# Router logits with the weights as the stationary operand, in a strip of 16 of 128 columns, and two transposes per half of the tokens

## The reference

```python
x = x + tanh(g_xattn) * xattn(layernorm(x), ctx, mask, W, b)
h = layernorm(x)
logits = h @ w_router                      # 2048 x 8
top_logits, top_idx = top_k(logits, 2)
scores = softmax(top_logits)
# each token goes to its 2 experts: silu(h @ fc1[:, :256]) * (h @ fc1[:, 256:]) @ fc2
moe = sum over the 2 experts of scores * expert(h)
shared = silu(h @ gate_w) * (h @ up_w) @ down_w      # inner width 512
x = x + tanh(g_ffn) * (moe + shared)
```

## Time and profile before

| what | value |
|---|---|
| three timed runs | 239.44, 240.22, 240.24 us (median 240.22) |
| span of the profiled execution | 237.5 us |
| median of the runs less that span | 2.7 us |
| PE busy | 222.3 us, 94% |
| DVE / ACT / POOL busy | 72% / 55% / 53% |
| TensorE clock in the profile's slices | 9 tenths or more in all 40 |

### The profile page before, as it was taken

The page is one execution under the profiler, slowest core; times in us unless marked ns, Lnnn a source line. Parts: engine busy times, 40 slices in busy tenths (PEclk is TensorE's granted clock), DMA queues, the critical chain, the costliest instruction groups (busy, mean ns, idle before and its releaser), DMA issues.

```text
span 237.5 us, 5283 instructions
## 1 busy us (share of the span) xinstructions
PE 222.3 (94%) x1425; PEld 193.7 (82%) x1425; DVE 171.8 (72%) x513; ACT 129.8 (55%) x316; POOL 125.1 (53%) x177
## 2 busy tenths in 40 slices
PE   7688999999989999999599999999999999999984
PEld 7578999978778888888488888888888888888763
DVE  0977897797767799999977665665665665664794
ACT  2465788773647645464125656656656656655320
POOL 1688898464777887887701334334334334334600
PEclk9999999999999999999999999999999999999999
DMA  5999950000121225322242443343343332008877
GB/s 154 286 362 406 404 199 3 0 0 25 45 94 67 74 85 179 136 91 92 67 123 65 135 127 94 96 125 96 88 127 92 94 120 68 37 38 267 288 238 310
DMA packets 18131, 32.05 MB, mean 135 GB/s; under 512 B 3046, under 2 KB 9323, under 8 KB 18104
## 3 DMA queue, kind: packets, MB, share of 16 engines
q1 hardware_dynamic: 14096, 22.28, 29.8%
q0 software_dynamic: 3408, 8.46, 9.5%
q10 hardware_dynamic: 600, 0.97, 1.3%
HBM read 19.95 MB, written 12.67 MB: 137 GB/s over the span
## 4 chain that ended last, share of the span: by engine, by line
PE 46%; POOL 8%; issue 6%; DMA 2%; DVE 2%; SPq 0%; DVEq 0%; ACT 0%; POOLq 0%
PE bank L994 38%; POOL rows L388 6%; PE bank L1245 4%; PE bank L1265 3%; POOL ew_lo L243 2%; DMA rows<-hrows,slot 1%; DMA hrows<-rows 1%; DVE act_lo L630 1%; DVE acc L710 0%; PE bank L1179 0%; DVE act L929 0%; DVE acc L966 0%; SPq L280 0%; ACT act L581 0%; DVEq L62 0%
## 5 line engine op out<-in xcount | busy, mean ns | idle before, releaser
L430 POOL DMA_INDIRECT parts<-y_out,dst x39 | 38.7, 991 | 69.9 <-DVE dst L923 66.1
L388 POOL DMA_INDIRECT rows<-hrows,slot x32 | 35.0, 1095 | 12.3 <-issue 12.3
L929 DVE TENSOR_TENSOR act<-act,bank 128x256 f32<-128x256 f32 x39 | 16.4, 421 | 34.5 <-issue 25.0
L581 ACT ACTIVATE act<-bank 128x256 f32<-128x256 f32 x39 | 15.0, 384 | 37.1 <-PE bank L994 37.1
L994 PE MATMUL bank<-ew_hi,m_xt_hi 128*128 x78 | 30.9, 396 | 0.1
L994 PE MATMUL bank<-ew_hi,m_xt_lo 128*128 x78 | 30.8, 395 | 0.0
L994 PE MATMUL bank<-ew_lo,m_xt_hi 128*128 x78 | 30.7, 394 | 0.0
L994 PE MATMUL bank<-ew_hi,act_hi 128*128 x78 | 25.2, 323 | 0.1
L994 PE MATMUL bank<-ew_hi,act_lo 128*128 x78 | 21.9, 281 | 0.0
L994 PE MATMUL bank<-ew_lo,act_hi 128*128 x78 | 21.9, 281 | 0.0
L443 ACT ACTIVATE act_hi<-act 128x512 fp32r<-128x512 f32 x16 | 10.1, 630 | 21.2 <-DVE act L690 9.1
(11 more groups left out here) (186 smaller groups left out, 655.6 us busy)
## 6 DMA issues: line engine op xcount, KB each, us to landing
ew_raw<-in_chunks SPq DMA_DIRECT2D x12, 512.0 KB, 10.7
hrows<-rows SPq DMA_DIRECT2D x39, 130.0 KB, 2.1
low_buf<-parts SPq DMA_DIRECT2D x4, 512.0 KB, 4.6
high_buf<-parts SPq DMA_DIRECT2D x4, 512.0 KB, 3.9
acc<-in_x SPq DMA_DIRECT2D x7, 256.0 KB, 4.6
sw_raw<-in_chunks SPq DMA_DIRECT2D x3, 512.0 KB, 9.0
out<-acc SPq DMA_DIRECT2D x3, 512.0 KB, 3.0
rows<-pad_rows SPq DMA_DIRECT2D x9, 130.0 KB
```

What stands on the lines that cost most here:

```text
L388: pool.indirect_dma_start(out=rows, out_offset=bass.IndirectOffsetOnAxis(ap=slot[:, h, k, i:i + 1], axis=0), in_=hrows[:, HT * h + i, :], ...
L430: pool.indirect_dma_start(out=parts, out_offset=bass.IndirectOffsetOnAxis(ap=dst[:, t:t + 1], axis=0), in_=y_out[:, t % SLOTS, :], in_offs ...
L581: a.activation(act[:, p, 0:I], M_H[p][:, 0:I], ACT.Silu).then_inc(s["m_sil"], 1)
L929: TT(act[:, p, 0:I], act[:, p, 0:I], M_H[p][:, I:2 * I], ALU.mult).then_inc(s["m_prod"], 1)
```

## The change

The router weights become the stationary operand. `wr` is widened from 16 to 176 columns per half of the features (WZ is 48), all zeros but for 16 columns in the middle; POOL writes the zeros at the start. For the group at place `at_` (0 to 3) in its half a window of 128 columns of it is taken, so that the 16 weight columns lie at 16 x `at_`. The 256 tokens of the group move past it, once as `ht_hi` and once as `ht_lo`, for each of the two halves of the features: four matmuls of 256 columns a group. All four groups of a half add into the same 128x256 of bank 6, each into its own 16 partitions, since the others' columns are zero there.

The logits then lie with experts on partitions and tokens along the row. DVE copies the 64x256 of them to SBUF (`cut_logits`), the PE turns them with two transposes (`turn_logits`), and DVE reads the turned ones (`read_logits`), now with an index order of its own. `turn_logits(0)` stands within `gate(0)`, behind its first three matmuls, and `turn_logits(1)` within `gate(3)`. `cut_logits(0)` takes the place of `read_logits(0)`, and that moves behind `softmax_out(6)`.

```diff
+HG = NG // NH
+WZ = 2 * E * (HG - 1)
...
-        wr = sb("wr", [P, K, 2 * E], F32R)
+        wr = sb("wr", [P, K, WZ + P], F32R)
+        lgt = sb("lgt", [HG * 2 * E, GN])
...
+            pool.memset(wr[:].bitcast(F32), 0.0).then_inc(s["wr_z"], 1)
             pool.wait_ge(s["const_m"], 1)
...
-            hi(wr[:, :, 0:E], wr_raw, "wr_h")
+            after(a, "wr_z", 1)
+            hi(wr[:, :, WZ:WZ + E], wr_raw, "wr_h")
...
-            lo(wr[:, :, E:2 * E], wr_raw, wr[:, :, 0:E], "wr_l")
+            lo(wr[:, :, WZ + E:WZ + 2 * E], wr_raw, wr[:, :, WZ:WZ + E], "wr_l")
...
+            def cut_logits(h):
+                after(v, "lg_ps", HG * (h + 1))
+                after(v, "lg_turned", h)
+                v.tensor_copy(lgt[:], bank[6][0:HG * 2 * E, 0:GN]).then_inc(s["lg_cut"], 1)
+
             def read_logits(h):
-                after(v, "lg_ps", (NG // NH) * (h + 1))
-                lp = bank[6][:, HT * h * 2 * E:HT * (h + 1) * 2 * E].rearrange("p (t e) -> p t e", e=2 * E)
-                v.tensor_copy(lgx[:], lp).then_inc(s["lg_read"], 1)
+                after(v, "lg_turned", h + 1)
+                lp = bank[6][:, GN:GN + HT * 2 * E].rearrange("p (j g e) -> p g j e", j=GT, g=HG)
+                v.tensor_copy(lgx[:].rearrange("p (g j) e -> p g j e", j=GT), lp).then_inc(s["lg_read"], 1)
...
                 if t == NG - 1:
                     after(v, "const_c", 7)
-                    read_logits(0)
+                    cut_logits(0)
                 softmax_out(t - 1)
...
                 if t == NG - 1:
+                    read_logits(0)
                     first_choice(0)
...
+            cut_logits(1)
             read_logits(1)
...
             def router(g):
                 after(pe, "ht_l", g + 1)
+                at_ = g % HG
+                if at_ == 0:
+                    after(pe, "lg_cut", g // HG)
+                w_ = slice(WZ - 2 * E * at_, WZ - 2 * E * at_ + P)
+                for k in range(K):
+                    for x_ in (ht_hi, ht_lo):
+                        ins = pe.matmul(bank[6][:, 0:GN], wr[:, k, w_], x_[:, k, g * GN:(g + 1) * GN],
+                                        start=at_ == 0 and k == 0 and x_ is ht_hi,
+                                        stop=at_ == HG - 1 and k == K - 1 and x_ is ht_lo, skip_group_check=True)
+                ins.then_inc(s["lg_ps"], 1)
+
+            def turn_logits(h):
+                after(pe, "lg_cut", h + 1)
+                after(pe, "lg_read", h)
+                n_ = HG * 2 * E
                 for j in range(GT):
-                    i = GT * g + j
-                    at_ = i * 2 * E
-                    for k in range(K):
-                        pe.matmul(bank[6][:, at_:at_ + 2 * E], ht_hi[:, k, i * P:(i + 1) * P], wr[:, k, :],
-                                  start=k == 0, stop=False, skip_group_check=True)
-                        ins = pe.matmul(bank[6][:, at_:at_ + E], ht_lo[:, k, i * P:(i + 1) * P], wr[:, k, 0:E],
-                                        start=False, stop=k == K - 1, skip_group_check=True)
-                ins.then_inc(s["lg_ps"], 1)
+                    ins = pe.transpose(bank[6][:, GN + j * n_:GN + (j + 1) * n_], lgt[:, j * P:(j + 1) * P],
+                                       ident[0:n_, 0:n_])
+                ins.then_inc(s["lg_turned"], 1)
...
+            def gate_around_logits(n, h):
+                after(pe, "ht_l", (SN // GN) * (n // FC + 1))
+                after(pe, "chunk_lp", 4)
+                after(pe, "prod", n - 1)
+                fs, gs = slice(n % FC * P, n % FC * P + P), slice(n // FC * SN, (n // FC + 1) * SN)
+                for k in range(K):
+                    for i, (x_, y_) in enumerate(((sw_hi, ht_hi), (sw_hi, ht_lo), (sw_lo, ht_hi))):
+                        ins = pe.matmul(GU[n % 2][0][:], x_[:, k, fs], y_[:, k, gs], start=k == 0 and i == 0,
+                                        stop=k == K - 1 and i == 2, skip_group_check=True)
+                    if k == 0:
+                        turn_logits(h)
+                ins.then_inc(s["gate_ps"], 1)
...
-            gate(0)
+            gate_around_logits(0, 0)
...
-            gate_up(3)
+            gate_around_logits(3, 1)
+            up(3)
```

More of the change, by code:

```diff
@@ L198, in build @@
             xt_ps xt_h xt_l wt_h wt_l y_h y_l xp_ps xp sc_ps sc_in sc_max sc_exp eT_ps eT_h eT_l mt_ps s_inv resid stats2 mean2 pre2 pow2 rstd2 h_ready
-            hT_ps ht_h ht_l lg_ps lg_read rt picked rank_ps placed wts low_expert w_sign w_tanh fields slots t_expm scattered pads tb tiles_known
+            hT_ps ht_h ht_l wr_z lg_ps lg_cut lg_turned lg_read rt picked rank_ps placed wts low_expert w_sign w_tanh fields slots t_expm scattered pads tb tiles_known
             chunk_h chunk_lp chunk_lv gate_ps up_ps sil prod act_h act_l dn_ps dn_added
```

## The result

The changed kernel takes 243.05 us (median of 4 runs, 242.73 to 243.21), the kernel before 240.23 beside it (239.44 to 240.41): ratio 1.0131, 95% interval 1.0108 to 1.0154. It is slower by 2.8 us. The forecast was 241.7, its range ended at 242.5: the sign was right and the size half of what came. The profiled execution took 242.9, of which 241.2 is span. In all that follows, executions more than 1.5% above the fastest of the same kernel (one of the kernel before, one of e3, two of e7) are left out of the ratios.

What follows compares the result with a forecast made beforehand. POOL's scatter queue, not the busy PE, was taken as the bound. Round trip 1.08 and collision 1.95, less A 0.82, then smaller returns, gave p 1.58 and the end 1.5 later: span 239.0, plus 2.7, 241.7 us; range 239.5 to 242.5.

Steps and rivals of the forecast that it cites:

- Router and first phase: Eight router groups at 0.48 us each instead of 0.89; DVE's own cycle leaves a first-phase pass 0.23 us of slack.
- A: How much earlier DVE is in pass 7 of the first phase: 0.82 us, bounds nothing and 1.23.
- Round trip: Logits copied, turned on the PE, read back: choice starts 1.08 us later on DVE's clock; bounds 0.8 and 1.4.
- T: Start of the new cut_logits on DVE, 47.14 on the clock of before; the choice was to begin 1.38 us later.
- Collision: First choice's DVE instructions with two SBUF inputs wait out POOL's cuts: 1.95 of 3.03 us late; chance 0.42.
- one slip: Rival: L755 of the first choice gets between POOL's cuts; p about 1.0, 241.2 us; chance 0.20, with milder collisions.
- p: Shift of POOL's point at 58.41 us, where it waits for the statistics of group 6; forecast 1.58 us later.
- From there the PE works through: matched(6) 2.21 us late, then PE works on to rank_first, some 0.2 of waiting gone: ranking 2.0 us late.
- From p to the end: POOL's later points move with p, less 0.05 at gate(3); 0.69 us idle at 72.06 stays; end 1.5 us later.
- No collision: Rival: first choice's DVE instructions lose nothing to POOL's cuts; p = -0.15, 240.0 us, not slower; chance 0.17.
- The PE as the bound after all: Rival: first phase gains the full 1.23 us, round trip 0.8, collision absent; 239.4 us; chance 0.08.
- That the gain in the first phase doesn't come: Rival: an unseen wait binds, A = 0.3 with the collision; p = 2.1, 242.3 us; chance 0.13, shared with another case.

Runs made afterwards that it cites:

- e3: Changed kernel with eight useless 512-column matmuls ahead of matched(6), collision left in; 241.05 us, ratio 1.0051 to the kernel before.
- e7: Changed kernel with POOL's two weight cuts moved off the first choice and up(0) ahead of matched(6); 239.37 us, ratio 0.9971 to the kernel before.
- e1: Changed kernel with POOL's two weight cuts moved off the first choice, one earlier, one given to DVE; 239.69 us, ratio 0.9985 to the kernel before.
- e8: e7 with cut_logits(0) put ahead of DVE's statistics of group 5; 238.71 us, ratio 0.9947 to the kernel before.
- e2: Kernel before, old router, with the same move of POOL's two cuts as e1; 239.48 us, ratio 0.9987 to the kernel before.
- e9: Kernel before, old router, with POOL's two cuts moved and up(0) ahead of matched(6); 238.42 us, ratio 0.9949 to the kernel before.
- e4: Changed kernel with up(0), six useful matmuls, moved ahead of matched(6), collision left in; 240.95 us, ratio 1.0048 to the kernel before.
- e5: Changed kernel with ten useless 512-column matmuls in the PE's idle ahead of the first tile; 242.29 us, ratio 1.0122 to the kernel before.
- e6: Changed kernel unaltered, measured again later; 242.69 us, ratio 1.0152 to the kernel before.
- e11: e7 without cut_logits and the transposes, DVE reading the logits as if turned; 238.07 us, ratio 0.9923 to the kernel before.
- e10: e8 with the ten useless matmuls of e5 ahead of the first tile; 239.15 us, ratio 0.9987 to the kernel before.

## Why the prediction came out wrong

**The base.** The span was to be 239.0 and is 241.2, 2.2 too low; the time was too low by only 1.35. The rest is in the 2.7 us held constant: all profiled executions here have 1.7 to 1.8 between span and time, so that the profiled execution of before must have been one of about 239.2, a microsecond under its median. The 80 runs of the kernel before that the experiments were compared with go with the clock: the 41 with a mean clock of 0.997 or more have a median of 239.3, the 34 from 0.99 to 0.997 240.1, the five below it 241.0. The trace of before is one without a half-clock stretch, and a median over runs of all three kinds isn't. Such a stretch also comes where the PE has hardly been idle: the traces of e1 and e8 have the granted clock at 0.50 from about 19 to 21 us, in a dense part of the first phase, and their DVE reaches the logits 1.3 to 1.4 us later for it. The window of e1:

```profile
19.00:22.00 3.00, 3.00 (x17) 3.00 (x16) 2.73 (x11) 1.12 (x5) 2.54 (x7) 0.50 1.06 409
```

One more part of the spread is when an execution gets going: POOL's first root is at 5.57 to 6.45 in the profiles.

**Router and first phase: right.** 0.57 a group, forecast 0.48 with a first gap not reckoned. A pass takes 4.94 (38.64 to 43.58), before 5.19: 0.25, forecast 0.23 of slack. DVE is at the logits 1.23 earlier, of which 0.45 was there at the start already (POOL's first root at 5.88, before at 6.33): 0.78, forecast A = 0.82. The other profiles agree: from POOL's first root to DVE at the logits is 40.79 to 40.81 us with the old router (before, e2, e9), 39.92 to 40.03 with the new one (all but e1 and e8, with their early stretch at half clock). Of the 2.6 us that the routers gave back (an estimate, eight times the 0.32 of one group) this is what arrived.

**Round trip: right in kind, 0.24 too dear.** T to L771 took 1.14, forecast 1.38. Its three steps are 0.44 to the PE (46.35), 0.37 back to DVE (46.72) and 0.33 to the choice (47.05). The third was right; the first was reckoned 0.49 and the second 0.54, from the last modelled end of a pair of transposes and a handover behind it, where DVE goes on sooner.

**Collision: right, one instruction off.** With the choice 0.24 earlier L764 slipped ahead of the cut, and L765 and L767 were the two that waited. The choice was done 1.67 late (50.21 for 48.99, and the 0.45) in place of 2.21. That is the rival "one slip", put at p about 1.0 and 241.2 us; e7 against e4 prices the collision at 1.8 us. The prediction named a sign against itself: with L764 (before, L754) at 0.23 in the first choice the collision was to be wrong and the time near 240. L764 took 0.23, and the collision came all the same, in the two instructions behind it. The Trainium skill's page "SBUF — State Buffer", section "Who interferes with whom", says that the shared pair of ports is an exclusive lock, held for the whole instruction. L765 and L767 agree with that, each ending just behind one cut. What a waiting instruction does between cuts in a row the case shows both ways: L765 got in between two, and the row of 4420 ns waited out three.

**"From there the PE works through": wrong.** This is the step that failed. `matched(6)` to `rank_first` was to take 2.9, at 0.23 a 512-column matmul. It took 4.41 and 5.25 in the two profiles of the changed kernel, because the PE had just stood idle 2.35 us, and its next 3.4 us or more were granted at half clock. The prediction had that idle in its own numbers: `matched(6)` 2.21 late on top of 0.42 is 2.6 us of nothing to do. It asked who is late next, and not what an idle PE costs afterwards. e3 shows it: the same collision, the idle filled, 2.83, and 1.0051 where the unfilled kernel is at 1.0131 and 1.0152. So p came to 2.36 net of the head start (60.32 - 58.41 + 0.45), forecast 1.58: `matched(6)` 0.54 less late, the stretch behind it 1.5 longer (4.41 for 2.9), and 0.2 less in what follows. In e5 (2.29) and e6 (3.38), which have the same idle, p reckoned in this way is about as large or larger; in e3, with the idle filled, it is 0.82, so that filling it takes 1.54 off. The sixteen runs of these three measurements have a mean clock of 0.993 at most; eight of the 24 of e3 and e4 reach 0.997. That the idle brings the fall is so by these profiles, three of three; why it falls is not shown, and e1 and e8 show a fall that no long idle goes ahead of.

**From p to the end: right, with a gap.** POOL's three points moved as one (1.91, 1.88, 1.99), with 0.66 of idle at 73.94 as foretold. Missing from the sum were the 0.81 at half clock at the first tile, in one profile of two, and the other course of e6, where a second collision at 106.8 uses up the 2.4 us of slack. That PE time saved after 70 us only widens the 2.46 holds for one course alone.

**The rivals.** No collision: e1 and e7, 239.7 and 239.4; that is at or just under the 240.0 reckoned for it. The PE as the bound after all: fell as a gain, since e9 with the eight dearer routers is not shown slower than e7. That the gain in the first phase doesn't come fell too: 0.78 of 0.82 came. "The change doesn't do what it says": fell with the rows at 40.19 to 40.55. The turning, which I put at little once the collision was gone, counts nearly in full in e11's trace, because the PE then waits for the picks.

## What to carry to other kernels

Where an edit shifts two engines against each other whose instructions hold each other up, lay their new times side by side, instruction by instruction: net of the head start the choice here began only 0.06 us late (47.05 and 0.45, before 47.44), but POOL's cuts had come 0.79 earlier (47.63 and 0.45, before 48.87), and the meeting cost 1.8. If the sum then shows the PE idle for some two microseconds, as here 2.35, price what follows at half clock too, and fill the gap with work that has to be done anyway. Time saved on the busiest engine is worth what the chain of waits gives for it: 2.6 us of router bought 0.78, and the round trip that it needs took 0.84.

## What the runs showed of the hardware

- After 2.34 to 2.35 us without a matmul near 50 us the PE did its first work at full clock or none of it, and then 3.4 us and more at 0.50 to 0.54, the 1.2 GHz level, though busy throughout: three profiles of three (after, e5, e6). After a similar idle of 2.36 to 2.46 us at the first tile the clock fell in three profiles (after, e8, e11) and stayed whole in five (before, e2, e4, e7, e9). After 0.97, 0.68 and 0.49 us (e4, e1, e3) it stayed whole.
- A long idle is not the only thing that goes ahead of half clock. In e1 the granted clock was 0.50 from 19 to 22 us and in e8 from 19 to 21, though it had been 1.00 from 6 to 18 us, and the PE's longest idle of the nine microseconds before was 0.51 us; the profile after and the others have that idle too, and no fall. What brought it is open.
- Useless matmuls during the flight of an indirect scatter went with a landing of 3.75 and 4.03 us in place of 2.90 to 3.00 without them (e5 and e10; one profile each). The cause is open.
- Beside two cuts of POOL in a row (48.91 and 50.14 their ends) two DVE instructions with both inputs in SBUF took 1.17 and 0.93 us for 0.22, and ended 0.08 and 0.07 behind the one and the other cut.
